# Attention weights turned in 32x32 blocks by VectorE and moved by DMA, in place of TensorE transposes

## The reference

```python
normed = _layernorm(hidden, g1, b1)
q, k, v = normed @ Wq + bq, normed @ Wk + bk, normed @ Wv + bv      # split into 8 heads of 32
logits = einsum('bhnd,bhmd->bhnm', q, k) / sqrt(32) + (2.0 * adj - 1.0)
weights = softmax(logits, axis=-1) * (0.25 + 0.75 * adj)
weights = weights / maximum(weights.sum(axis=-1), 1e-06)
hidden = hidden + einsum('bhnm,bhmd->bhnd', weights, v) @ Wo + bo
ff = gelu(_layernorm(hidden, g2, b2) @ Wf1 + bf1) @ Wf2 + bf2
x = hidden + ff
# second layer, twice: layer norm, h = x @ W, e = leaky_relu(s_i + t_j) + adj,
# softmax over j, sum over j of the weights times h, plus x
```

## Time and profile before

| | |
|---|---|
| profiled execution | 1125.41 us |
| span | 1123.6 us |
| TensorE busy | 1070.8 us (95%) |
| VectorE busy | 772.3 us (69%) |
| ScalarE busy | 713.8 us (64%) |
| GpSimd busy | 408.0 us (36%) |
| moved by DMA | 32.10 MB, mean 29 GB/s |

### The profile page before, as it was taken

One profiled execution on the slowest core, in us unless ns is written; L12 is line 12 of the kernel. 1 busy time (PEld: TensorE's weight loads), 2 busy tenths in 40 slices (PEclk: granted clock), 3 DMA queues, 4 the chain that ended last, 5 costly groups with the idle time before them and its releaser, 6 DMA issues.

```text
span 1123.6 us, 38526 instructions
## 1 busy us (share of the span) xinstructions
PE 1070.8 (95%) x16172; PEld 945.3 (84%) x16172; DVE 772.3 (69%) x1889; ACT 713.8 (64%) x1718; POOL 408.0 (36%) x628
## 2 busy tenths in 40 slices
PE   5999999999999989999999999999999999979997
PEld 5888888888888868899889998998888888868886
DVE  4577777677776767754455445545788888859996
ACT  2777767777677755543555345536688788857774
POOL 3431121121121113332223222322387777775662
PEclk9999999999999999999999999999999999989999
DMA  7001101111100001000000000000010001002122
GB/s 225 30 30 58 32 31 31 30 31 59 30 13 2 3 27 33 1 1 1 1 1 1 1 1 1 1 1 11 11 33 22 23 23 33 3 3 73 61 76 94
DMA packets 41804, 32.10 MB, mean 29 GB/s; under 512 B 5280, under 2 KB 41376, under 8 KB 41632
## 3 DMA queue, kind: packets, MB, share of 16 engines
q1 hardware_dynamic: 37312, 29.36, 8.2%
q10 hardware_dynamic: 4320, 0.28, 0.3%
HBM read 21.25 MB, written 8.39 MB: 26 GB/s over the span
## 4 chain that ended last, share of the span: by engine, by line
PE 71%; POOL 11%; issue 9%; DVE 6%; ACT 2%; ACTq 1%; POOLq 0%; DVEq 0%
PE BK L1235 8%; PE BK L1237 8%; PE BK L1236 8%; PE BK L1373 6%; PE BK L1461 5%; PE BK L1462 5%; PE BK L1463 5%; PE BK L1347 5%; PE BK L1359 4%; PE BK L1340 3%; POOL x_all L938 3%; POOL x_all L849 3%; PE BK L1260 3%; POOL atc L930 2%; POOL rstd L870 1%
## 5 line engine op out<-in xcount | busy, mean ns | idle before, releaser
L1088 ACT ACTIVATE gf<-BK,bcol 128x512 f32<-128x512 f32 x128 | 88.1, 689 | 182.7 <-PE BK L1237 167.4
L868 POOL TENSOR_TENSOR ve<-mv,eps_l 128x4 f32<-128x4 f32 x64 | 15.4, 240 | 438.7 <-DVE mv L289 405.8
L1004 ACT ACTIVATE e_sb<-BK,nmx 128x128 f32<-128x128 f32 x512 | 141.5, 403 | 28.3 <-DVE nmx L455 28.3
L1461 PE MATMUL BK<-wf_hi,gh 128*128 128x256 f32 x512 | 143.5, 280 | 0.0
L1462 PE MATMUL BK<-wf_hi,gl 128*128 128x256 f32 x512 | 141.8, 277 | 0.0
L1463 PE MATMUL BK<-wf_lo,gh 128*128 128x256 f32 x512 | 141.7, 277 | 0.0
L546 DVE TENSOR_TENSOR gl<-gf,gh 128x512 fp32r<-128x512 f32 x128 | 93.4, 731 | 62.9 <-ACT gh L1089 61.1
L461 DVE TENSOR_TENSOR pt_sb<-BK,ft 128x512 f32<-128x512 f32 x128 | 85.2, 686 | 70.1 <-PE BK L1347 68.5
L1024 ACT ACTIVATE xn<-x_all,neg_mr,rstd 128x256 f32<-128x256 f32 x188 | 103.8, 611 | 5.2 <-POOL neg_mr L877 4.8
L1237 PE MATMUL BK<-xh,wf_lo 128*128 128x512 f32 x256 | 100.8, 394 | 0.0
L1236 PE MATMUL BK<-xl,wf_hi 128*128 128x512 f32 x256 | 100.6, 393 | 0.0
(11 more groups left out here) (204 smaller groups left out, 2869.7 us busy)
## 6 DMA issues: line engine op xcount, KB each, us to landing
x_all<-in_x_dram SPq DMA_DIRECT2D x16, 512.0 KB, 4.1
adj_in<-in_adj_dram SPq DMA_DIRECT2D x32, 256.0 KB, 2.9
out_dram<-y SPq DMA_DIRECT2D x16, 512.0 KB, 3.0
s_wf<-in_L_gnn_Wf_dram SPq DMA_DIRECT2D x2, 1024.0 KB, 9.9
s_w<-in_L_gnn_W_dram SPq DMA_DIRECT2D x2, 256.0 KB, 2.9
s_wq<-in_L_gnn_Wq_dram SPq DMA_DIRECT2D x1, 256.0 KB, 5.7
s_wk<-in_L_gnn_Wk_dram SPq DMA_DIRECT2D x1, 256.0 KB, 6.3
s_wv<-in_L_gnn_Wv_dram SPq DMA_DIRECT2D x1, 256.0 KB, 8.0
```

The source lines that it names most:

```text
L1004: e = act.activation(e_sb[:, j, :], LE[:, r, q, :], ACT.Exp, bias=nmx[:, j:j + 1], scale=1.0)
L1088: act.activation(gf[f % 2][:], BK[:, f % 4, :], ACT.Gelu, bias=bcol[:, 6 + f:7 + f])
L1461: pe.matmul(dst, gh[:, f, n], hi[:, f, :], start=(f == 0), stop=False)
```

## The change

It replaces the way in which a matrix gets its other axis onto the partitions, in three places.

Attention. GpSimd multiplies the exponentials, still with the query on the partition, with the mask's factor, in place in e_sb (a_weigh, four instructions a pair). VectorE transposes them in 32x32 blocks into the buffer tb (a_turn, four instructions a pair): each block is turned, but stays in its own group of 32 partitions. The sync queue then moves the blocks to the right partitions with 16 transfers a pair (move_turned), each of 32 partitions with 2 KB, into pt_sb. The mask's factor is made from the mask as it is loaded, so adj_turn is gone. tb lies where w1 comes later. The products with v are made further behind: a_av takes graphs 2 sp - 5 and 2 sp - 4 in the half chunk of pair sp, where it was 2 sp - 2 and 2 sp - 1. For that v has three buffers. The semaphore a_ld counts the moves, 256 a pair.

Feed-forward. The next chunk's normalised input is made at f = 3 instead of 4, block-turned by VectorE (block_turn) and moved by 16 transfers of 32 partitions with two runs of 512 bytes, onto xn itself; ScalarE and VectorE make xh and xl from there (turned_hi, turned_lo), VectorE behind the second graph. The last chunk still uses ln_turn.

Masks. In feed-forward chunks 2 to 9 the sync queue loads the masks for the graph layer in rearranged 32x32 blocks (load_blocks, runs of 128 bytes), VectorE turns two of them a chunk, and they are stored to the DRAM tensor adj_kept; the first graph layer loads them from there.

```diff
-            def a_pt_out(sp, par, pp, r):
-                dve.wait_ge(a_tt, sp * 4 + (r + 1))
-                f = ft_sb[par][:, 2 * pp:2 * pp + 2, :].unsqueeze(2).to_broadcast([P, 2, KT, P])
-                dve.tensor_tensor(pt_sb[pp][:, 4 * r:4 * r + 4, :].rearrange("p (g t) n -> p g t n", t=KT),
-                                  LE[:, r].rearrange("p (g t) n -> p g t n", t=KT), f, ALU.mult).then_inc(a_pt, 1)
+            def a_turn(sp, r):
+
+                dve.wait_ge(a_pm, sp * 4 + (r + 1))
+                wait_for(dve, a_ld, sp * 256)
+                heads = slice(4 * r, 4 * r + 4)
+                dve.transpose(tb[:, :, heads, :], e_sb[:, heads, :].rearrange("p j (b n) -> p b j n", n=32)).then_inc(a_tb, 1)
...
+            def block_turn(c):
+
+                dve.wait_ge(ln_xn, (c + 1) * G)
+                wait_for(dve, ln_ld, (c - CB - 1) * 256)
+                blocks = xn[:].rearrange("p g (b n) -> p b g n", n=32)
+                for kt in range(KT):
+                    dve.transpose(tb_ln[:, 4 * kt:4 * kt + 4, :].rearrange("p b (g n) -> p b g n", g=G),
+                                  blocks[:, 4 * kt:4 * kt + 4]).then_inc(ln_t, 1)
...
                     if sp >= 0:
                         a_max(sp, 0)
...
                     if sp >= 0:
                         a_max(sp, 1)
+                    if s >= 5:
+                        a_norm(s - 5)
+                    if sp >= 1:
+                        a_turn(sp - 1, 2)
+                        a_turn(sp - 1, 3)
+                    if s >= 6:
+                        a_resid(s - 6)
+                    if pp == 1 and i < NC:
                         a_ft_out(i, par)
...
+                    if sp >= 0:
+                        a_turn(sp, 0)
...
+                    if s >= 4:
+                        a_norm(s - 4)
+                    if sp >= 0:
+                        a_turn(sp, 1)
...
+            def move_turned(sp_):
+
+                gate(a_tb, sp_ * 4 + 4)
+                gate(a_o, 2 * sp_ - 2)
+                for b in range(4):
+                    for a in range(4):
+                        sp.dma_start(pt_sb[sp_ % 2][32 * b:32 * b + 32, a], tb[32 * a:32 * a + 32, b]).then_inc(a_ld, 16)
+
+            def a_step(i, half, par):
+                if i >= 2:
+                    move_turned(2 * i - 3)
...
+                if i + 2 < NC:
+                    load_x(i + 2)
+                if i + 1 < NC:
+                    load_adj(i + 1)
...
+                if i >= 1:
+                    move_turned(2 * i - 2)
...
+            def b_step(i, half, par):
+
+                if i < NC - 1:
+                    gate(ln_t, (i + CB + 2) * KT)
+                    for q in range(4):
+                        for a in range(4):
+                            sp.dma_start(turned[32 * q:32 * q + 32, :, a, :],
+                                         tb_ln[32 * a:32 * a + 32, q:8:4, :]).then_inc(ln_ld, 16)
+                if 2 <= i < 2 + NC // 2:
+                    for j in (2 * i - 4, 2 * i - 3):
+                        keep_adj(j)
+                        if j + 2 < NC:
+                            load_blocks(j + 2)
...
+            def a_weigh(sp_, r):
+
+                pool.wait_ge(a_ft, sp_ // 2 + 1)
+                pool.wait_ge(a_e, sp_ * 4 + (r + 1))
+                f = ft_sb[sp_ // 2 % 2][:, 2 * (sp_ % 2):2 * (sp_ % 2) + 2, :].unsqueeze(2).to_broadcast([P, 2, KT, P])
+                e = e_sb[:, 4 * r:4 * r + 4, :].rearrange("p (g t) n -> p g t n", t=KT)
+                pool.tensor_tensor(e, e, f, ALU.mult).then_inc(a_pm, 1)
...
+            def turned_hi(c):
+                act.wait_ge(ln_ld, (c - CB) * 256)
+                for kt in range(KT):
+                    act.activation(by_graph(xh[:, kt, :]), turned_rows(kt), ACT.Copy).then_inc(ln_xh, 1)
...
-            def a_turn(sp, r):
-                pe.wait_ge(a_e, sp * 4 + (r + 1))
-                for q in range(4):
-                    m = pe.transpose(LE[:, r, q, :], e_sb[:, 4 * r + q, :], ident[:])
-                m.then_inc(a_tt, 1)
...
+            def a_av(s):
+
+                sp_, c = s // 2, s // G
+                if s % 2 == 0:
+                    pe.wait_ge(a_vev, c * 2 + 2)
+                    pe.wait_ge(a_ld, (sp_ + 1) * 256)
```

More of the change, by code:

```diff
@@ L492, in a_step, with a_aggr @@
+            def a_aggr(c):
+                dve.wait_ge(ln_st, (c + CA + 1) * G)
+                wait_for(dve, ln_nm, nm_count(c - 1, CA))
+                aggr(c + CA)
             def a_step(i, half, par):
-                first, tail = (isinstance(i, int) and i == n for n in (0, NC))
                 for pp in range(2):
[L495 to L498, removed]
+                    sp = i * 2 + (pp - 2)
+                    s = 2 * sp
+                    if sp >= 0:
@@ L499, in a_step @@
                         a_max(sp, 0)
-                    if pp == 0 and not first:
+                    if pp == 0 and i > 0:
                         ln_lo(i + CA)
-                    if not first:
+                    if sp >= 0:
                         a_max(sp, 1)
[L504 to L509, removed]
@@ L510, in a_step @@
-                    if pp == 0 and not tail:
-                        a_ft_out(i, par)
[L512 to L529, removed]
-            chunks(dve, a_step)
-            a_step(NC, NC // 2, 0)
-            a_norm(NG - 2)
-            a_resid(NC - 1, 1, NG - 3)
@@ L539, in b_step @@
+                    if pp == 1 and i <= NC - 2:
+                        a_aggr(i + 2)
+            chunks(dve, a_step, NC + 1)
+            a_norm(NG - 5)
+            a_turn(NG // 2 - 1, 2)
+            a_turn(NG // 2 - 1, 3)
+            for s in range(NG - 6, NG - 1):
+                a_resid(s)
+                if s + 2 < NG:
+                    a_norm(s + 2)
+            a_resid(NG - 1)
             def b_step(i, half, par):
@@ L555, in b_step @@
                         setup_constants()
-                    if f == 4:
+                    if f == 3:
                         normalise(i + CB + 1, nxt)
+                        if not final:
+                            block_turn(i + CB + 1)
+                    if f == 5 and 2 <= i < 2 + NC // 2:
+                        if i == 2:
+                            dve.wait_ge(setup_act, 4)
+                            dve.wait_ge(setup_pool, 13)
+                        adj_turn(2 * i - 4)
+                        adj_turn(2 * i - 3)
+                    if f == 5 and i == 3 + NC // 2:
+                        for r in range(2):
+                            dve.wait_ge(adj_st[r], NC // 2 * 16)
                     if final and f == 5:
@@ L819, in _ @@
                 sp.dma_start(a_bc[n][:], a.rearrange("h k -> (h k)").partition_broadcast(P)).then_inc(w_l1, 16)
+            def b_step(i, half, par):
[10 more added lines that the diff above has]
+                            load_blocks(j + 2)
+            chunks(sp, b_step)
+            for r in range(2):
+                gate(adj_st[r], NC // 2 * 16)
             load_c(0, 0, CC)
@@ L889, in norms @@
                         add_bias(i, CB, bf2_bc, b_xb)
-                    if first == CA and not (isinstance(i, int) and i == 0):
-                        add_bias(i, CA, bo_bc, a_xb)
                     if first == CD:
@@ L1376, in a_step @@
             def a_step(i, half, par):
-                first, tail = (isinstance(i, int) and i == n for n in (0, NC))
                 for pp in range(2):
-                    s, sp = i * G + (2 * pp - G), i * 2 + (pp - 2)
-                    back = not (isinstance(s, int) and s < 2)
-                    old = not (isinstance(s, int) and s < 3)
-                    before = (i - 2, par, 1) if pp == 0 else (i - 1, 1 - par, 0)
-                    if isinstance(i, int) and i == 1 and pp == 1:
+                    sp = i * 2 + (pp - 2)
+                    s = 2 * sp
+                    if i == 1 and pp == 1:
                         pe.wait_ge(setup_dve, setup_at["biases"])
-                    if not first:
+                    if sp >= 0:
                         a_logits(sp, i - 1, 1 - par, pp)
```

401 lines of the change are left out of this document (231 added, 170 removed).

## The result

| | before | after |
|---|---|---|
| median of the runs, us | 1127.13 (4 runs, 1126.33 to 1128.47) | 1525.12 (4 runs, 1521.63 to 1535.25) |
| profiled execution, us | 1125.4 | 1521.63 |
| its span, us | 1123.6 | 1519.8 |
| attention stage ends (w load issued) | 417.2 | 775.6 |
| the rest of the span | 706.4 | 744.2 |

The ratio is 1.3533 (95%: 1.3481 to 1.3584). The forecast was 1397 with a range of 1285 to 1490: the side was right, the size was 128 us short, and the time lies outside the range.

What follows compares the result with a forecast made beforehand. TensorE bounded the kernel before; a closed loop through the one buffer tb would bind attention after. 1125.4 + 284 (attention) - 10 (feed-forward) - 4 (graph layer) = 1395, median 1.6 above the profiled execution: 1397 us, range 1285 to 1490.

Steps and rivals of the forecast that it cites:

- its own signs: Attention: VectorE idle 8 to 9 us before each pair's first a_turn, 31 times; TensorE idle 6 to 9, clock 0.5 behind.
- T: Attention, fourth block turn done until 16 transfers are issued and landed: 9.3 us a pair, bounds 7.8 to 11.5.
- V: Attention, VectorE from a pair's first block turn to its fourth: mean 11.2 us, 8.9 at full clock.
- Stage end: Attention ends at 701 us, 284 later than before, with 31 periods of 20.5 us a pair.
- Feed-forward: Eight transposes fewer in 15 chunks: 10 of 13 us gained, bounds 13 gained and 18 lost.
- chain of 22.1: Feed-forward: normalisation, block turns, T, copies and low part end 22.1 us after chunk start, just fitting a 22.4 us chunk.
- Graph layer: First graph layer: four transposes fewer in 16 chunks, 4 of 7 us gained, as GpSimd is near its limit as well.
- the ends don't come together: Whole kernel: summed bounds give 1247 and 1529 us; the range was set at 1285 to 1490.
- Rival 3: Attention: issues cost next to nothing or transfers land before VectorE returns to a_turn; T 2.3, 1109 us; chance 4%.
- Rival 4: Attention: the wait for the moves doesn't bind and TensorE stays the bound; 1043 us at best; chance 2%.
- rival 2: Sync queue: issues slow to 1.1 us apart with many transfers in flight, T 19, 1830 us; chance 5%.
- Rival 1: Attention: TensorE's clock holds, period 18.2 us a pair, stage end 630, 1326 us; chance 15%.

Runs made afterwards that it cites:

- e3: Changed kernel with a second buffer tb for the turned exponentials, each with its own landing semaphore: 1220.62 us, ratio 1.0813 to the kernel before.
- e2: Changed kernel with 8 of the 16 moves of a pair in attention left out, so half the turned exponentials stay unmoved: 1359.68 us.
- e4: Changed kernel with the same 16 moves a pair in attention, each with a quarter of its bytes: 1509.4 us.
- e8: Changed kernel with the same count of attention moves and bytes, each over all 128 partitions with 512 bytes (wrong data arrives): 1526.4 us.
- e11: Changed kernel with 40 unused matmuls a pair in TensorE's gap ahead of the transposes that wait for the norm: 1493.55 us.
- e1: Changed kernel with the feed-forward input turned by TensorE again, attention and turned masks as changed: 1487.17 us, ratio 1.3174 to the kernel before.
- e6: Changed kernel with 24 unused matmuls a pair in TensorE's gap ahead of the transposes that wait for the norm: 1533.13 us.

## Why the prediction was right in kind and wrong in size

- **What binds.** Right, by its own signs: 31 waits before the first a_turn of a pair, released by the moves, TensorE idle before a_attn_turn, the clock at 0.50 behind it. The waits were longer than forecast, 11.5 us on VectorE for 8 to 9 and 10.2 on TensorE for 6 to 9. e3 shows that the one buffer is the cause: with a second one a pair takes 12.9 us in place of 23.0.
- **T, the step that failed.** The prediction priced an issue at 0.47 from one pair of loads, and "I take it to be per instruction". The second half holds (e2, e4, e8). The first doesn't carry over: the moves start 0.663 apart. T was 12.2 for 9.3, above the forecast's upper bound of 11.5, and 2.9 x 31 = 90 us. The landing, 2.0, was right. Part of it could have been read before the result. The first of those two loads came after a pause, and they are not equal, 0.37 us for 256 KB and 0.45 for 512. At the start of the trace of before, loads stand directly behind one another:
```profile
1.91 0.50 SPq L780 DMA_DIRECT2D s_wq<-in_L_gnn_Wq_dram  x1
2.45 0.47 SPq L780 DMA_DIRECT2D s_wk<-in_L_gnn_Wk_dram  x1
2.96 0.47 SPq L780 DMA_DIRECT2D s_wv<-in_L_gnn_Wv_dram  x1
3.47 0.54 SPq L781 DMA_DIRECT2D wo_sb<-in_L_gnn_Wo_dram  x1
4.05 1.02 SPq L773 DMA_DIRECT2D x_all<-in_x_dram  x1
```
They start 0.51 to 0.58 apart, 0.535 in the mean; at that price T is 10.3. The other 0.13 an issue no row of before shows: 0.10 is what the moves cost over such loads, 0.03 are the few issues over 0.9 us.
- **V.** 10.65 for 11.2, -0.55 x 31 = -17 us. The block turn cost 0.70 for 0.65. The clock's part was at least 1.3 for 2.3 (e11), so the rest of V was up to 0.4 longer than forecast.
- **Stage end.** 701 + 90 - 17 = 774, measured 775.6. Two sizes were off in opposite directions, so a part of T's miss was covered by luck.
- **Feed-forward.** +38 us (e1) where -10 was forecast, from three terms. First T: with 12.1 in place of 9.3 the forecast's own chain of 22.1 becomes 24.9, and the first 14 chunks are 24.9 us apart, 23.0 before the change: 26.5 us. Second, the chunk before was taken as 23.3; most are 22.8, so that without the transposes TensorE has 21.9 and the chain of 22.1 did not fit even at T 9.3. Third, a term that the sum doesn't have: the last but one chunk takes 34.0 us for 25.5 before. TensorE's set-up for the graph layer (L1433, L1448) waits there until VectorE has made the low parts, which now come behind the moves, and the fourth graph's products stand behind the set-up, so work that lay beside the chain comes after it, from 1149.3 to 1158.1, and costs 8.5 us:
```profile
1149.34 1.65 PE L1433 MATMUL BK<-cols,wc 128*128 128x1 f32 x8 [4.61 <-DVE xl L335]
1150.85 3.76 PE L1448 MATMUL BK<-s_w,lb_wide 128*128 128x256 f32 x8
...
1158.12 0.40 PE L1402 MATMUL BK<-xh,wf_hi 128*128 128x512 f32 x1
```
Together that is 35 us; the last 3 lie behind feed-forward. The normalisation began 7.8 us into the chunk, forecast 7.7.
- **Graph layer.** Forecast -4, measured 0 (e1). The earlier trace rows had TensorE at 98% and VectorE and GpSimd at 86% and 77%; relieving the first brought nothing.
- **Sum.** 1395 + 73 + 48 + 4 = 1520 for the profiled execution, measured 1521.6.
- **The range.** Its upper end came from T 11.5, turns 1.0 and feed-forward late together, 1529 (its own terms make some 10 us more), cut to 1490 because "the ends don't come together". One price, that of an issue, moves T in both stages at once, so two of the three did come together. Smaller slips decide nothing: rivals 3 and 4 have 6% together where "faster" has 4%, and rival 2's terms add up to 1838 and not 1830.
- **Rivals.** Rival 1 fell: the clock did not hold (0.75 in the stage). Rival 2 (issues take longer when many are in flight) has a grain of truth: in e3, with the queue always full, issues over 0.9 us are more than twice as many, but most cost the same. Rival 3 needed 0.04 us an issue. Rival 4 fell with the 31 waits.

## What to carry to other kernels

Count the DMA instructions of a transfer that is cut into pieces, and multiply by the queue's price per issue, taken where issues stand directly behind one another and for the same kind of source and destination. If a single buffer closes the loop, that product and one landing are paid in full in every round. A second buffer turned the latency into throughput of the queue (1525 to 1221 us); a share on another engine's queue, together with feed-forward as it was before, made 1140, and the loads ahead of the moves 1117. That is 1% under the kernel before: once the moves are out of the way, taking 63 us of transposes off TensorE in attention was worth 4. A filler that is meant to hold the clock proves nothing where idle time is left behind it, as the 4.08 us of e6.

## What the runs showed of the hardware that was not expected

- A transfer from SBUF to SBUF takes 0.59 to 0.60 us to issue on the sync queue when it stands directly behind another (0.61 to 0.62 on ScalarE's), 0.63 to 0.64 from start to start, with 64 KB or 16, 32 partitions or 128. The first move of a pair takes 0.51 (0.46 in e8).
- The recurring loads and stores between DRAM and SBUF on the same queue of the changed kernel take 0.32 to 0.51 us (medians). Four of 64 KB over 32 partitions in a row start 0.524 apart.
- About one issue in 27 takes over 0.9 us, up to 2.0, and one in 11 when the queue has hardly a pause (e3). In the changed kernel all 19 are among the second to the tenth of their 16, 18 of them among the second to the sixth; why is open.
- A block turn of 128x512 takes VectorE 0.70 us; a product in place on GpSimd of the same size 1.28 us, where the earlier trace rows had 1.46 for another product.
